# A list of its own for the first batch: who accumulates y in units 0 to 12

## The chip, the cores and the metric

One core of a Trainium2 chip. The metric is the device time of one execution, in microseconds (us); lower is better. The engines of the core are named as the profile names them: PE (TensorE, with PEld its weight loads), DVE (VectorE), ACT (ScalarE), POOL (GpSimd) and SP (SyncE, which here only issues DMAs).

## The reference

Four batches of 512 time steps go through a selective state-space layer beside a gated feed-forward layer. Cut to what matters here (D = 1024 channels, N = 16 states, H = 512):

```python
xn = layernorm(x)
u, gate = split(xn @ W_in.T); u = silu(causal_conv(u))
dt, B, C = rmsnorm each of split(u @ Wx.T)
delta = softplus(dt @ Wdt.T + dt_bias)
state[d, n] = exp(delta[d] * A[d, n]) * state[d, n] + delta[d] * u[d] * B[n]   # for each time step
y[d] = sum over n of state[d, n] * C[n]
s = ((y + u * D_param) * silu(gate)) @ W_out.T
g = silu(down(silu(gate_ffn(xn)) * up(xn)))
out = x + s * g
```

The change touches only who adds up the sum over n that gives y.

## The kernel before

The batches run one after the other: batch 0 written out on its own, batches 1 and 2 in a loop, batch 3 written out on its own (`sequences`). Inside a batch the scan is cut into 32 **units** (`UNITS`): unit i is state n = i mod 16 of channel half i // 16, which is four tiles of 128 channels by 512 time steps. A unit has two **slots**, so a batch has 64 slots, and every engine's program is written slot by slot with other work (feed-forward, projections, the next batch's preparation) placed in fixed slots.

What one unit costs on each engine:

- POOL makes `dBu` = v times B, one instruction per slot (L794), into a ring of three buffers: the one of slot s waits for the scans of slot s - 3.
- ACT makes the decays `dA` = exp(delta A) in PSUM, two per slot (L584).
- DVE scans, two per slot (L1018): `dA` and `dBu` in, the state `h` out. It waits for both.
- PE transposes `h` back to time-major, 128 time steps (an index c from 0 to 3) at a time, into two PSUM banks hT0 (c = 0 and 2) and hT1 (c = 1 and 3) (L1364). c = 0, 1 go in the unit's first slot and c = 2, 3 in its second, and each waits until the bank's former contents were read. PE's slots run one to two behind DVE's, because the first waits for all four scans of its unit.
- y, in `yT`, gets hT times C[n] added. DVE does it in one instruction per c (`add_state`, L947; L941 where n = 0), in the two slots of the next unit, behind that slot's scans and ahead of its other work. For some (unit, c) it is **handed over**: ACT multiplies the bank by C[n] into a buffer `part` of SBUF (`take_state`, L677; with n = 0 straight into `yT`), and POOL adds that to `yT` (`add_part`, L764), four slots after the unit's start.

`handed_over(u)` says which: c = 0 of nearly all units, and c = 2 as well in units 11 to 22. The same list holds for all four batches. OFF is the list of these, OFF_ADDS those of them with n > 0, ON all others; counts of them (`done_by`) are the values that the semaphores ev_done (ACT), yp_done (POOL) and y_done (DVE) are waited for.

Batch 0 differs from the others in one thing: the weights that feed the fp32r products (x is multiplied in a high and a low part, L1079) are split there, once, and kept in DRAM for the later batches. ACT rounds an entry to its high part (`round_w`, L449) and POOL subtracts to get the low part (`rest_w`, L733). 15 entries are split inside the slots of batch 0: on POOL in the even slots 2 to 26, then in slots 33 and 36. PE's product of slot 2t (feed-forward, t = 0 to 10) waits for the low part made in POOL's slot 2t + 2. In slots 14, 16, 18 and 20 POOL has one more instruction of 128x1024 each (L744 or L749, for the second channel half), and in slot 25 eleven short ones for the next batch's layer norm (L702 to L719).

Of the kernel before, what the change touches and what calls it, by code (L numbers as in the profile page):

```python
# [11 lines left out]
JH = KD // HF  # L12
UNITS = N * HF
# [70 lines left out]
def done_by(acts, u, c):  # L84

    return len([a for a in acts if a <= (u, c)])

# [45 lines left out]
def build(nc, x, w_ring, w_x, w_dt, conv_w, conv_b, a_par, d_par, ln_w, ident_d, out):  # L133
# [5 lines left out]
    with ctx:  # L139
# [287 lines left out]
        def _(act):  # L427
# [146 lines left out]
            def sequence(b, first, last):  # L574
# [88 lines left out]

                def take_state(c_b, i, c, no_first):

                    hf, n = i // N, i % N
                    act.wait_ge(hT_ps, c_b * UNITS * TC + i * TC + c + 1)
                    if n == 0:
                        if not no_first:
                            act.wait_ge(yb_ps, (c_b - 1) * KD + (hf + 1) * JH)  # L670
                        dst = yT[:, c, hf * JH * P:(hf + 1) * JH * P]
                    else:
                        q = OFF_ADDS.index((i, c))
                        if not (no_first and q < 2):
                            act.wait_ge(yp_done, c_b * len(OFF_ADDS) + q - 1)
                        dst = part[:, q % 2, :]
                    nc.scalar.activation(dst, hT[c % H_BANKS][:, :], ACT.Copy, scale=cs_act[:, c, n:n + 1]).then_inc(ev_done, 1)  # L677

                for s in range(SLOTS):
                    decay(s)  # L680
                    side(s)
                    for i, c in OFF:
                        if s == 2 * i + 2 + c // 2:
                            take_state(b, i, c, first)
                        elif s == 2 * i + 2 + c // 2 - SLOTS and not first:
                            take_state(b - 1, i, c, False)
# [9 lines left out]
        def _(pool):  # L696
# [57 lines left out]

            def add_part(c_b, i, c):
                q, hf = OFF_ADDS.index((i, c)), i // N
                pool.wait_ge(ev_done, c_b * len(OFF) + done_by(OFF, i, c))
                before = [p for p in range(q) if OFF_ADDS[p][1] == c and OFF_ADDS[p][0] // N == hf]
                if (i - 1, c) in ON:
                    pool.wait_ge(y_done, c_b * len(ON) + done_by(ON, i - 1, c))  # L760
                elif before:
                    pool.wait_ge(yp_done, c_b * len(OFF_ADDS) + before[-1] + 1)
                y = yT[:, c, hf * JH * P:(hf + 1) * JH * P]
                nc.gpsimd.tensor_tensor(y, y, part[:, q % 2, :], ALU.add).then_inc(yp_done, 1)  # L764

# [11 lines left out]
            def sequence(b, first, last):  # L777
                for s in range(SLOTS):
# [20 lines left out]
                    if s in LO_AT and first:  # L799
                        o, k = LO_AT[s]  # L800
                        rest_w(slot_of(b, k), o % HI_RING, split(k))
                    for m, c in OFF_ADDS:
                        if s == 2 * m + 4 + c // 2:
                            add_part(b, m, c)
                        elif s == 2 * m + 4 + c // 2 - SLOTS and not first:
                            add_part(b - 1, m, c)
                    j = s - S_YB1 - 7 + JH
# [25 lines left out]
            sequences(pool, sequence)  # L833
            for m, c in OFF_ADDS:
                if SLOTS <= 2 * m + 4 and m < UNITS - 1:
                    add_part(NB - 1, m, c)
            for j in range(JH, KD):
# [3 lines left out]
        def _(dve):  # L841
# [91 lines left out]
            def sequence(b, first, last):  # L933
                def add_state(c_b, i, c):
# [3 lines left out]
                    dve.wait_ge(hT_ps, c_b * UNITS * TC + i * TC + c + 1)  # L938
                    if n == 0:
                        dve.wait_ge(cs_done, c_b + 1)  # L940
                        nc.vector.tensor_scalar(y, hT[c % H_BANKS][:, :], cn, None, ALU.mult).then_inc(y_done, 1)  # L941
                    else:
                        if (i - 1, c) in ON:
                            dve.wait_ge(y_done, c_b * len(ON) + done_by(ON, i - 1, c))
                        else:
                            dve.wait_ge(yp_done, c_b * len(OFF_ADDS) + done_by(OFF_ADDS, i - 1, c))
                        nc.vector.scalar_tensor_tensor(out=y, in0=hT[c % H_BANKS][:, :], scalar=cn, in1=y,  # L947
                                                       op0=ALU.mult, op1=ALU.add).then_inc(y_done, 1)
# [3 lines left out]
                def side(s):  # L952
                    if first and 1 <= s < 3:
                        gate_silu(0, s + 1, pj[s - 1])
                    if s == 1 and not first:
                        dve.wait_ge(y_done, b * len(ON))
                        hand_c(b)
# [54 lines left out]
                for s in range(SLOTS):  # L1012
                    i, part = s // 2, s % 2
                    dve.wait_ge(dBu_done, b * SLOTS + s + 1)
                    for e in range(2):
                        g = 2 * s + e
                        dve.wait_ge(dA_done, b * SCANS + g + 1)
                        nc.vector.tensor_tensor_scan(h[:, i % 2, 2 * part + e, :], dA[g % 2][:, :], dBu[:, dbu_buffer(s), e, :],  # L1018
                                                     0.0, ALU.mult, ALU.add).then_inc(scan_done, 1)
                    for c in (2 * part, 2 * part + 1):  # L1020
                        if i > 0 and (i - 1, c) in ON:
                            add_state(b, i - 1, c)
                        elif i == 0 and not first and (UNITS - 1, c) in ON:
                            add_state(b - 1, UNITS - 1, c)
                    side(s)
# [3 lines left out]
            for c in range(TC):  # L1029
                i = UNITS - 1  # L1030
                dve.wait_ge(hT_ps, b * UNITS * TC + i * TC + c + 1)
                if (i - 1, c) in ON:
                    dve.wait_ge(y_done, b * len(ON) + done_by(ON, i - 1, c))
                else:
                    dve.wait_ge(yp_done, (b + 1) * len(OFF_ADDS) - len(handed_over(i)) - len(handed_over(i - 1)) + done_by([(i - 1, d) for d in handed_over(i - 1)], i - 1, c))
                y = yT[:, c, JH * P:D]
# [13 lines left out]
        def _(pe):  # L1050
# [88 lines left out]
            def sequence(b, first, last):  # L1139
# [209 lines left out]
                for s in range(SLOTS):  # L1349
# [3 lines left out]
                    for c in (2 * part, 2 * part + 1):  # L1353

                        before = (i, c - H_BANKS) if c >= H_BANKS else (i - 1, c + TC - H_BANKS)
                        if not first or before[0] >= 0:
                            if last and before[0] == UNITS - 1:
                                pe.wait_ge(y_done, b * len(ON) + done_by(ON, UNITS - 2, TC) + before[1] + 1)
                            elif before in ON or (UNITS - 1, before[1]) in ON and before[0] < 0:
                                pe.wait_ge(y_done, b * len(ON) + (done_by(ON, *before) if before[0] >= 0 else done_by(ON, UNITS - 1, before[1]) - len(ON)))  # L1360
                            else:
                                pe.wait_ge(ev_done, b * len(OFF) + (done_by(OFF, *before) if before[0] >= 0 else done_by(OFF, UNITS - 1, before[1]) - len(OFF)))
                        for j in range(JH):
# [24 lines left out]
            for c in range(TC):  # L1388

                pe.wait_ge(y_done, b * len(ON) + done_by(ON, UNITS - 2, TC) + c + 1)  # L1390
                for j in (JH, JH + 1):
# [76 lines left out]
```

## Time and profile before

| | |
|---|---|
| median of 3 runs | 1181.65 us (1178.9 to 1184.5) |
| profiled execution | 1188.98 us, its span 1186.9 us |
| busy: PE, DVE, POOL, ACT | 90%, 86%, 86%, 60% of the span |
| slots of batch 0 | from 65 us to 358 us |
| granted TensorE clock, mean | 0.961 |

The start of DVE's scans tells where a slot lies in the trace: slot 4 at 87.20 us, slot 12 at 121.82, slot 14 at 131.57, slot 21 at 169.19, slot 28 at 200.86, slot 34 at 224.52. A timeline row gives start, duration of the row's instructions together (one begins a little before the one ahead of it has ended, so the distance of starts is the smaller price), the engine, line, tiles, shapes, the count, and in brackets how long the engine had been idle and what ended that.

### The profile page before, as it was taken

To read this page: it belongs to the slowest core of one execution; us is meant where nothing else is said; L and a number is where in the kernel's file an instruction comes from. 1 tells how busy PE (TensorE), PEld (TensorE's weight loads), DVE (VectorE), ACT (ScalarE), POOL (GpSimd) and SP (SyncE) were. 2 spreads that over 40 slices of the span, in tenths; PEclk is the share of its full clock that TensorE was granted. 3 is DMA by queue.
4 is the path that set the end of the run, shared out by engine and by line. 5 is a ranking of instruction groups with operands and counts; after the bars stand their busy time and mean duration, and the time that the engine had idled before them with its cause. 6 is when DMAs were issued, how large, how long until landed. Compare 5 with 4: busy or idle time off the path is not lost.

```text
span 1186.9 us, 16724 instructions
## 1 busy us (share of the span) xinstructions
PE 1070.9 (90%) x5072; PEld 766.5 (65%) x5072; DVE 1026.3 (86%) x1217; ACT 711.3 (60%) x1155; POOL 1016.0 (86%) x586
## 2 busy tenths in 40 slices
PE   5979987889999999998997999998998999999767
PEld 4747766666757776675855787576756777555444
DVE  3469788899789999899986999899998999888895
ACT  4657646776475756477583565576576575565440
POOL 3679999999878899889987789879998889889961
PEclk9979999799799999999998999999999999999878
DMA  3627654443223543343322364324333443334310
GB/s 126 214 94 242 215 169 159 147 146 133 63 90 140 190 164 141 132 151 134 99 90 101 133 215 163 131 98 157 118 100 105 162 155 130 109 114 169 124 62 36
DMA packets 46570, 160.86 MB, mean 136 GB/s; under 512 B 5355, under 2 KB 5611, under 8 KB 37004
## 3 DMA queue, kind: packets, MB, share of 16 engines
q1 hardware_dynamic: 45424, 159.14, 38.7%
q8 instruction: 44, 0.72, 0.2%
q10 hardware_dynamic: 1052, 0.59, 0.2%
q14 instruction: 50, 0.41, 0.1%
HBM read 135.33 MB, written 24.38 MB: 135 GB/s over the span
## 4 chain that ended last, share of the span: by engine, by line
PE 49%; DVE 17%; POOL 16%; issue 13%; ACT 3%; DVEq 1%; DMA 1%; SPq 0%; POOLq 0%; ACTq 0%
PE pj L1079 16%; PE hT L1364 10%; DVE sb_h L1018 8%; POOL sb_dBu L794 8%; PE pj L1277 7%; PE pj L1311 5%; DVE sb_yT L947 4%; PE pj L1342 3%; POOL sb_yT L764 3%; PE pj L1084 2%; PE pj L1382 2%; DVE sb_un L872 2%; PE pj L1097 2%; POOL sb_w_sp L733 1%; POOL sb_un L738 1%
## 5 line engine op out<-in xcount | busy, mean ns | idle before, releaser
L1018 DVE TENSOR_TENSOR_SCAN sb_h<-dA,sb_dBu 128x512 f32<-128x512 f32 x512 | 596.8, 1207 | 43.7 <-POOL sb_dBu L794 30.2
L794 POOL TENSOR_TENSOR sb_dBu<-sb_v,sb_bb 128x1024 f32<-128x1024 f32 x256 | 607.1, 2384 | 28.6 <-DVE sb_h L1018 22.8
L584 ACT ACTIVATE dA<-sb_delta,sb_apar 128x512 f32<-128x512 f32 x512 | 344.9, 688 | 232.4 <-DVE sb_h L1018 226.4
L1079 PE MATMUL pj<-sb_x_hi,sb_w_sp 128*128 128x512 f32 x1208 | 345.8, 410 | 25.4 <-DVE sb_un L872 12.3
L1364 PE MATMUL hT<-sb_ident,sb_h 128*128 128x128 f32 x2048 | 288.7, 283 | 66.8 <-DVE sb_yT L947 51.7
L1364 PEld LDWEIGHTS hT<-sb_ident,sb_h 128*128 128x128 f32 x2048 | 244.4, 145 | 149.9 <-issue 50.9
L1079 PEld LDWEIGHTS pj<-sb_x_hi,sb_w_sp 128*128 128x128 f32 x1208 | 221.2, 193 | 89.0 <-issue 24.6
L947 DVE SCALAR_TENSOR_TENSOR sb_yT<-hT,sb_cs,sb_yT 128x512 f32<-128x512 f32 x321 | 229.2, 735 | 53.8 <-PE hT L1364 53.2
L764 POOL TENSOR_TENSOR sb_yT<-sb_yT,sb_part 128x512 f32<-128x512 f32 x155 | 199.4, 1286 | 63.5 <-ACT sb_part L677 63.4
L677 ACT ACTIVATE sb_part<-hT,sb_cs_act 128x512 f32<-128x512 f32 x155 | 106.1, 685 | 161.4 <-PE hT L1364 152.9
L1079 PE MATMUL pj<-sb_x_lo,sb_w_sp 128*128 128x512 f32 x604 | 167.4, 400 | 0.0
L1079 PEld LDWEIGHTS pj<-sb_x_lo,sb_w_sp 128*128 128x128 f32 x604 | 117.4, 194 | 27.8
L1311 PE MATMUL pj<-sb_S,sb_ring 128*128 128x512 f32 x264 | 121.8, 598 | 0.0
L1277 PE MATMUL pj<-sb_u,sb_ring 128*128 128x512 f32 x192 | 86.6, 594 | 0.0
L1311 PEld LDWEIGHTS pj<-sb_S,sb_ring 128*128 128x128 f32 x264 | 46.8, 190 | 52.7 <-issue 52.7
L872 DVE SCALAR_TENSOR_TENSOR sb_un<-pj,sb_cw,sb_un 128x511 f32<-128x511 f32 (+2 forms) x93 | 69.5, 747 | 4.9 <-ACT sb_un L478 2.7
L733 POOL TENSOR_TENSOR sb_w_sp<-sb_ring,sb_w_sp 128x1024 fp32r<-128x1024 f32 x21 | 49.9, 2377 | 19.2 <-ACT sb_w_sp L449 19.2
L1277 PEld LDWEIGHTS pj<-sb_u,sb_ring 128*128 128x128 f32 x192 | 34.6, 190 | 35.0 <-issue 34.6
L753 POOL TENSOR_TENSOR sb_u<-sb_u,sb_sgate 128x512 f32<-128x512 f32 x32 | 41.4, 1297 | 11.3 <-DVE sb_u L899 11.3
L749 POOL TENSOR_TENSOR sb_v<-sb_delta,sb_un 128x1024 f32<-128x1024 f32 x16 | 38.1, 2383 | 8.7 <-DVE sb_delta L925 8.3
L744 POOL TENSOR_TENSOR sb_delta<-sb_delta,sb_v 128x1024 f32<-128x1024 f32 x14 | 33.4, 2388 | 11.1 <-ACT sb_v L534 11.1
L738 POOL TENSOR_TENSOR sb_un<-sb_v,sb_un 128x512 f32<-128x512 f32 x32 | 41.4, 1300 | 0.0
(126 smaller groups left out, 810.1 us busy)
## 6 DMA issues: line engine op xcount, KB each, us to landing
sb_w_sp<-w_cache SPq DMA_DIRECT2D x55, 1024.0 KB, 4.8
sb_ring<-w_ring SPq DMA_DIRECT2D x67, 512.0 KB, 3.3
sb_bb<-b_rows SPq DMA_DIRECT2D x128, 256.0 KB, 3.6
w_cache<-sb_w_sp SPq DMA_DIRECT2D x19, 1024.0 KB, 4.9
sb_xio<-x SPq DMA_DIRECT2D x7, 1024.0 KB, 6.9
out<-sb_xio SPq DMA_DIRECT2D x3, 1024.0 KB, 5.6
sb_xio<-x SPq DMA_DIRECT2D x4, 256.0 KB, 3.6
out<-sb_xio SPq DMA_DIRECT2D x4, 256.0 KB, 2.0
```

The lines of the kernel that those rows point to most:

```text
L584: nc.scalar.activation(dA[g % 2][:, :], delta[:, j, :], ACT.Exp, scale=apar[:, j, n:n + 1]).then_inc(dA_done, 1)
L677: nc.scalar.activation(dst, hT[c % H_BANKS][:, :], ACT.Copy, scale=cs_act[:, c, n:n + 1]).then_inc(ev_done, 1)
L733: nc.gpsimd.tensor_tensor(w_lo[:, buf], ring[:, slot], w_hi[:, buf].bitcast(fp32), ALU.subtract).then_inc(lo_done, 1)
L764: nc.gpsimd.tensor_tensor(y, y, part[:, q % 2, :], ALU.add).then_inc(yp_done, 1)
L794: nc.gpsimd.tensor_tensor(dBu[:, dbu_buffer(s), :, :], v[:, j:j + 2, :], bb[:, i % B_RING, :].unsqueeze(1).to_broadcast([P, 2, T]), ALU.mu ...
L872: nc.vector.scalar_tensor_tensor(out=acc[:, k:T], in0=bank[:, 0:T - k], scalar=cw[:, j, KC - 1 - k:KC - k], in1=acc[:, k:T], op0=ALU.mult, ...
L947: nc.vector.scalar_tensor_tensor(out=y, in0=hT[c % H_BANKS][:, :], scalar=cn, in1=y, op0=ALU.mult, op1=ALU.add).then_inc(y_done, 1)
L1018: nc.vector.tensor_tensor_scan(h[:, i % 2, 2 * part + e, :], dA[g % 2][:, :], dBu[:, dbu_buffer(s), e, :], 0.0, ALU.mult, ALU.add).then_in ...
L1079: done = nc.tensor.matmul(bank[:, :], w[:, kk * P:(kk + 1) * P], xs[:, kk, :], start=(p == 0), stop=(p == len(products) - 1))
L1277: done = nc.tensor.matmul(pj[e % 2][:, :], ring[:, slot_of(b, OUT0 + e), part, m * P:(m + 1) * P], u[:, j, :], start=(j == 0), stop=(j == ...
L1311: done = nc.tensor.matmul(pj[DOWN_BANK[e]][:, :], ring[:, slot_of(b, DOWN0 + x3 // 2), x3 % 2, t % 4 * P:(t % 4 + 1) * P], S[:, t, :], sta ...
L1364: done = nc.tensor.transpose(hT[c % H_BANKS][:, j * P:(j + 1) * P], h[:, i % 2, j, c * P:(c + 1) * P], ident[:, :])
```

## The change

`handed_over` gets a second argument, whether this is batch 0. There, units 0 to 12 hand nothing over: DVE does all four c of them. From unit 13 on, and in batches 1 to 3, the list is as it was. So in batch 0 fifteen pairs (c = 0 of units 0 to 12, c = 2 of units 11 and 12) move: 15 instructions of ACT and 14 of POOL go, 15 of DVE come. PE waits for y_done where it waited for ev_done. The rest of the diff is bookkeeping of the counts, which differ between batch 0 and the others now; in the loop they come to as many register instructions as before, give or take one. The buffer of `part` is now counted from the list's end.

```diff
-def handed_over(u):
-    return (0, 2) if 11 <= u < 23 else () if u in (29, 30) else (0,)
-
-
-OFF = [(u, c) for u in range(UNITS) for c in handed_over(u)]
-OFF_ADDS = [(u, c) for u, c in OFF if u % N > 0]
-ON = [(u, c) for u in range(UNITS) for c in range(TC) if (u, c) not in OFF]
+def handed_over(u, first):
+    return () if u in (29, 30) or first and u < FIRST_UNIT else (0, 2) if 11 <= u < 23 else (0,)
+
+
+FIRST_UNIT = 13
+OFF, OFF_ADDS, ON = {}, {}, {}
+for first in (True, False):
+    OFF[first] = [(u, c) for u in range(UNITS) for c in handed_over(u, first)]
...
+def total(acts, b):
+
+    return 0 if isinstance(b, int) and b == 0 else b * len(acts[False]) + len(acts[True]) - len(acts[False])
...
-                    for i, c in OFF:
+                    for i, c in OFF[first]:
                         if s == 2 * i + 2 + c // 2:
-                            take_state(b, i, c, first)
+                            take_state(i, c, False)
...
-                    for m, c in OFF_ADDS:
+                    for m, c in OFF_ADDS[first]:
                         if s == 2 * m + 4 + c // 2:
-                            add_part(b, m, c)
+                            add_part(b, m, c, False)
...
-                        if i > 0 and (i - 1, c) in ON:
-                            add_state(b, i - 1, c)
+                        if i > 0 and c not in handed_over(i - 1, first):
+                            add_state(i - 1, c, False)
```

POOL around slots 14 to 16 of batch 0 (L733 is the low part of the weights, L764 the addition to y, L744 and L749 the extra work of these slots, L794 the dBu of two slots). Before:

```order
L733 TENSOR_TENSOR sb_w_sp<-sb_ring,sb_w_sp 128x1024
L764 TENSOR_TENSOR sb_yT<-sb_yT,sb_part 128x512
L744 TENSOR_TENSOR sb_delta<-sb_delta,sb_v 128x1024
L794 TENSOR_TENSOR sb_dBu<-sb_v,sb_bb 128x1024 x2
L733 TENSOR_TENSOR sb_w_sp<-sb_ring,sb_w_sp 128x1024
L764 TENSOR_TENSOR sb_yT<-sb_yT,sb_part 128x512
L749 TENSOR_TENSOR sb_v<-sb_delta,sb_un 128x1024
```

POOL at the same place after the change (its lines are 17 to 20 further on in the file):

```order
L750 TENSOR_TENSOR sb_w_sp<-sb_ring,sb_w_sp 128x1024
L761 TENSOR_TENSOR sb_delta<-sb_delta,sb_v 128x1024
L814 TENSOR_TENSOR sb_dBu<-sb_v,sb_bb 128x1024 x2
L750 TENSOR_TENSOR sb_w_sp<-sb_ring,sb_w_sp 128x1024
L766 TENSOR_TENSOR sb_v<-sb_delta,sb_un 128x1024
```

The addition to y between the weights' low part and the next work is gone.

DVE in an even and an odd slot of the same place (the rows on sb_h are the scans, those on sb_S the feed-forward). Before:

```order
L1018 SCALAR_TENSOR_TENSOR sb_h<-dA,sb_dBu 128x512 x2
L947 SCALAR_TENSOR_TENSOR sb_yT<-hT,sb_cs,sb_yT 128x512
L964 SCALAR_TENSOR_TENSOR sb_S<-sb_S,pj 128x512
L1018 SCALAR_TENSOR_TENSOR sb_h<-dA,sb_dBu 128x512 x2
L947 SCALAR_TENSOR_TENSOR sb_yT<-hT,sb_cs,sb_yT 128x512 x2
L969 SCALAR_TENSOR_TENSOR sb_S<-sb_S,pj 128x512
```

DVE at the same place after the change:

```order
L1041 SCALAR_TENSOR_TENSOR sb_h<-dA,sb_dBu 128x512 x2
L970 SCALAR_TENSOR_TENSOR sb_yT<-hT,sb_cs,sb_yT 128x512 x2
L987 SCALAR_TENSOR_TENSOR sb_S<-sb_S,pj 128x512
L1041 SCALAR_TENSOR_TENSOR sb_h<-dA,sb_dBu 128x512 x2
L970 SCALAR_TENSOR_TENSOR sb_yT<-hT,sb_cs,sb_yT 128x512 x2
L992 SCALAR_TENSOR_TENSOR sb_S<-sb_S,pj 128x512
```

The even slot holds two accumulations where it held one; the new one, c = 0, stands ahead of c = 1.

PE in an odd slot, with what the instructions wait for. Before:

```order
L1364 MATMUL hT0<-sb_ident,sb_h 128x128 [waits ev_done]
L1364 MATMUL hT0<-sb_ident,sb_h 128x128 x3
L1364 MATMUL hT1<-sb_ident,sb_h 128x128 [waits y_done]
L1364 MATMUL hT1<-sb_ident,sb_h 128x128 x3
L1079 MATMUL pj0<-sb_x_hi,sb_w_sp 128x512 [waits fs_done]
```

PE at the same place after the change:

```order
L1391 MATMUL hT0<-sb_ident,sb_h 128x128 [waits y_done]
L1391 MATMUL hT0<-sb_ident,sb_h 128x128 x3
L1391 MATMUL hT1<-sb_ident,sb_h 128x128 [waits y_done]
L1391 MATMUL hT1<-sb_ident,sb_h 128x128 x3
L1102 MATMUL pj0<-sb_x_hi,sb_w_sp 128x512 [waits fs_done]
```

Nothing moved; bank hT0 is now waited for on DVE (y_done) and no more on ACT (ev_done).

## Rows read from the trace of the kernel before

**Rows 1.** The page's first part: span, and busy time by engine.
```profile
span 1186.9 us, 16724 instructions
PE 1070.9 (90%) x5072; PEld 766.5 (65%) x5072; DVE 1026.3 (86%) x1217; ACT 711.3 (60%) x1155; POOL 1016.0 (86%) x586
```

**Rows 2.** Busy time by stretch of batch 0; PEclk is the granted clock.
```profile
85.00:130.00 45.00, 45.00 (x230) 35.16 (x228) 39.13 (x46) 35.05 (x55) 41.95 (x21) 1.00 0.72 245
130.00:168.00 38.00, 31.73 (x148) 24.31 (x147) 28.30 (x34) 18.89 (x27) 38.00 (x19) 0.91 0.55 181
168.00:206.00 38.00, 31.08 (x160) 24.46 (x158) 33.49 (x40) 23.41 (x37) 37.53 (x30) 0.96 0.47 162
228.00:293.00 65.00, 58.16 (x282) 41.29 (x280) 64.30 (x76) 48.93 (x79) 65.00 (x41) 1.00 0.43 151
```

**Rows 3.** Timeline of POOL in slot 16.
```profile
139.65 2.36 POOL L733 TENSOR_TENSOR sb_w_sp<-sb_ring,sb_w_sp 128x1024 fp32r<-128x1024 f32 x1
141.98 1.27 POOL L764 TENSOR_TENSOR sb_yT<-sb_yT,sb_part 128x512 f32<-128x512 f32 x1
143.22 2.38 POOL L749 TENSOR_TENSOR sb_v<-sb_delta,sb_un 128x1024 f32<-128x1024 f32 x1
```

**Rows 4.** DVE's waits at 130:168, 168:206, 206:228: us, times, longest.
```profile
DVE sb_h L1018 <- POOL sb_dBu L794: 8.1, 3, 2.9
...
DVE sb_h L1018 <- POOL sb_dBu L794: 6.1, 3, 2.8
...
DVE sb_h L1018 <- POOL sb_dBu L794: 2.6, 1, 2.6
```

**Rows 5.** Timeline of DVE: slots 12, 13, 17, 26 and 27.
```profile
124.07 0.73 DVE L947 SCALAR_TENSOR_TENSOR sb_yT<-hT,sb_cs,sb_yT 128x512 f32<-128x512 f32 x1
...
127.42 2.34 DVE L1018 TENSOR_TENSOR_SCAN sb_h<-dA,sb_dBu 128x512 f32<-128x512 f32 x2 [2.03 <-ACT dA L584]
129.68 1.38 DVE L947 SCALAR_TENSOR_TENSOR sb_yT<-hT,sb_cs,sb_yT 128x512 f32<-128x512 f32 x2
...
147.98 2.34 DVE L1018 TENSOR_TENSOR_SCAN sb_h<-dA,sb_dBu 128x512 f32<-128x512 f32 x2 [2.88 <-POOL sb_dBu L794]
...
191.35 2.34 DVE L1018 TENSOR_TENSOR_SCAN sb_h<-dA,sb_dBu 128x512 f32<-128x512 f32 x2 [0.96 <-POOL sb_dBu L794]
...
197.24 2.34 DVE L1018 TENSOR_TENSOR_SCAN sb_h<-dA,sb_dBu 128x512 f32<-128x512 f32 x2 [2.30 <-POOL sb_dBu L794]
```

**Rows 6.** Timeline of ACT in slots 12 and 13.
```profile
124.65 0.67 ACT L677 ACTIVATE sb_part<-hT,sb_cs_act 128x512 f32<-128x512 f32 x1
125.33 1.28 ACT L584 ACT_TABLE_LOAD   x1
...
127.87 1.03 ACT L449 CAST sb_w_sp<-sb_ring 128x1024 fp32r<-128x1024 f32 x1
```

**Rows 7.** PE's first gap after 85 us; who waited for L947 (us, times).
```profile
130.55 1.22 PE L1364 MATMUL hT<-sb_ident,sb_h 128*128 128x128 f32 x8 [0.25 <-DVE sb_yT L947]
```
```profile
  PE hT L1364: 51.7, 37
```

**Rows 8.** Timeline from slot 32 to 34: ACT, POOL, DVE.
```profile
216.38 0.69 ACT L677 ACTIVATE sb_part<-hT,sb_cs_act 128x512 f32<-128x512 f32 x1 [1.31 <-PE hT L1364]
216.97 1.04 ACT L449 CAST sb_w_sp<-sb_ring 128x1024 fp32r<-128x1024 f32 x1
```
```profile
218.57 2.34 POOL L733 TENSOR_TENSOR sb_w_sp<-sb_ring,sb_w_sp 128x1024 fp32r<-128x1024 f32 x1
```
```profile
224.52 2.34 DVE L1018 TENSOR_TENSOR_SCAN sb_h<-dA,sb_dBu 128x512 f32<-128x512 f32 x2 [2.56 <-POOL sb_dBu L794]
```

**Rows 9.** Timeline of PE: the products with Wx in batch 0 and batch 1.
```profile
293.00 4.68 PE L1084 MATMUL pj<-sb_wx,sb_un 128*128 128x64 f32 x32 [1.37 <-POOL sb_un L738]
...
299.18 6.93 PE L1084 MATMUL pj<-sb_wx,sb_un 128*128 128x64 f32 x32
...
575.07 3.68 PE L1084 MATMUL pj<-sb_wx,sb_un 128*128 128x64 f32 x32
```

More of the change, by code:

```diff
@@ L71, with done_by, done_before @@
 LO_AT = {q + 2: (o, k) for o, k, q in MADE}
-def handed_over(u):
-    return (0, 2) if 11 <= u < 23 else () if u in (29, 30) else (0,)
-OFF = [(u, c) for u in range(UNITS) for c in handed_over(u)]
-OFF_ADDS = [(u, c) for u, c in OFF if u % N > 0]
-ON = [(u, c) for u in range(UNITS) for c in range(TC) if (u, c) not in OFF]
-def done_by(acts, u, c):
-    return len([a for a in acts if a <= (u, c)])
+def handed_over(u, first):
[4 more added lines that the diff above has]
+    OFF[first] = [(u, c) for u in range(UNITS) for c in handed_over(u, first)]
+    OFF_ADDS[first] = [(u, c) for u, c in OFF[first] if u % N > 0]
+    ON[first] = [(u, c) for u in range(UNITS) for c in range(TC) if (u, c) not in OFF[first]]
+def total(acts, b):
+    return 0 if isinstance(b, int) and b == 0 else b * len(acts[False]) + len(acts[True]) - len(acts[False])
+def done_by(acts, b, u, c):
+    return total(acts, b) + len([a for a in acts[isinstance(b, int) and b == 0] if a <= (u, c)])
+def done_before(acts, b, u, c):
+    return total(acts, b) - len([a for a in acts[False] if a > (u, c)])
 def dbu_buffer(s):
@@ L753, in times_gate, with add_part @@
                 nc.gpsimd.tensor_tensor(u[:, j, :], u[:, j, :], sgate[:, j, :], ALU.mult).then_inc(yg_done, 1)
[L755 to L760, printed above, removed]
+            def add_part(b, i, c, carried):
+                acts = OFF_ADDS[isinstance(b, int) and b == 0 and not carried]
+                q, hf = acts.index((i, c)), i // N
+                done = done_before if carried else done_by
+                pool.wait_ge(ev_done, done(OFF, b, i, c))
+                before = [a for a in acts[:q] if a[1] == c and a[0] // N == hf]
+                if i > 0 and c not in handed_over(i - 1, acts is OFF_ADDS[True]):
+                    pool.wait_ge(y_done, done(ON, b, i - 1, c))
                 elif before:
-                    pool.wait_ge(yp_done, c_b * len(OFF_ADDS) + before[-1] + 1)
+                    pool.wait_ge(yp_done, done(OFF_ADDS, b, *before[-1]))
                 y = yT[:, c, hf * JH * P:(hf + 1) * JH * P]
-                nc.gpsimd.tensor_tensor(y, y, part[:, q % 2, :], ALU.add).then_inc(yp_done, 1)
+                nc.gpsimd.tensor_tensor(y, y, part[:, (len(acts) - q) % 2, :], ALU.add).then_inc(yp_done, 1)
             power_ln(0)
@@ L937, in add_state @@
                     cn = cs[:, c, n:n + 1]
-                    dve.wait_ge(hT_ps, c_b * UNITS * TC + i * TC + c + 1)
+                    dve.wait_ge(hT_ps, b * UNITS * TC + (i - UNITS if carried else i) * TC + c + 1)
                     if n == 0:
-                        dve.wait_ge(cs_done, c_b + 1)
+                        dve.wait_ge(cs_done, b + 1)
                         nc.vector.tensor_scalar(y, hT[c % H_BANKS][:, :], cn, None, ALU.mult).then_inc(y_done, 1)
                     else:
-                        if (i - 1, c) in ON:
-                            dve.wait_ge(y_done, c_b * len(ON) + done_by(ON, i - 1, c))
+                        done = done_before if carried else done_by
+                        if c not in handed_over(i - 1, first and not carried):
+                            dve.wait_ge(y_done, done(ON, b, i - 1, c))
+                        elif (i - 1) % N == 0:
+                            dve.wait_ge(ev_done, done(OFF, b, i - 1, c))
                         else:
-                            dve.wait_ge(yp_done, c_b * len(OFF_ADDS) + done_by(OFF_ADDS, i - 1, c))
+                            dve.wait_ge(yp_done, done(OFF_ADDS, b, i - 1, c))
                         nc.vector.scalar_tensor_tensor(out=y, in0=hT[c % H_BANKS][:, :], scalar=cn, in1=y,
@@ L955, in side @@
                     if s == 1 and not first:
-                        dve.wait_ge(y_done, b * len(ON))
+                        dve.wait_ge(y_done, total(ON, b))
                         hand_c(b)
@@ L1020, in sequence @@
                     for c in (2 * part, 2 * part + 1):
-                        if i > 0 and (i - 1, c) in ON:
-                            add_state(b, i - 1, c)
-                        elif i == 0 and not first and (UNITS - 1, c) in ON:
-                            add_state(b - 1, UNITS - 1, c)
+                        if i > 0 and c not in handed_over(i - 1, first):
+                            add_state(i - 1, c, False)
+                        elif i == 0 and not first and c not in handed_over(UNITS - 1, False):
+                            add_state(UNITS - 1, c, True)
                     side(s)
@@ L1031, in _ @@
                 dve.wait_ge(hT_ps, b * UNITS * TC + i * TC + c + 1)
-                if (i - 1, c) in ON:
-                    dve.wait_ge(y_done, b * len(ON) + done_by(ON, i - 1, c))
+                if c not in handed_over(i - 1, False):
+                    dve.wait_ge(y_done, done_by(ON, b, i - 1, c))
                 else:
-                    dve.wait_ge(yp_done, (b + 1) * len(OFF_ADDS) - len(handed_over(i)) - len(handed_over(i - 1)) + done_by([(i - 1, d) for d in handed_over(i - 1)], i - 1, c))
+                    dve.wait_ge(yp_done, done_by(OFF_ADDS, b, i - 1, c))
                 y = yT[:, c, JH * P:D]
@@ L1357, in sequence @@
                             if last and before[0] == UNITS - 1:
-                                pe.wait_ge(y_done, b * len(ON) + done_by(ON, UNITS - 2, TC) + before[1] + 1)
-                            elif before in ON or (UNITS - 1, before[1]) in ON and before[0] < 0:
-                                pe.wait_ge(y_done, b * len(ON) + (done_by(ON, *before) if before[0] >= 0 else done_by(ON, UNITS - 1, before[1]) - len(ON)))
+                                pe.wait_ge(y_done, done_by(ON, b, UNITS - 2, TC) + before[1] + 1)
+                            elif before[0] < 0 and before[1] in handed_over(UNITS - 1, False):
+                                pe.wait_ge(ev_done, done_before(OFF, b, UNITS - 1, before[1]))
+                            elif before[0] < 0:
+                                pe.wait_ge(y_done, done_before(ON, b, UNITS - 1, before[1]))
+                            elif before[1] in handed_over(before[0], first):
+                                pe.wait_ge(ev_done, done_by(OFF, b, *before))
                             else:
-                                pe.wait_ge(ev_done, b * len(OFF) + (done_by(OFF, *before) if before[0] >= 0 else done_by(OFF, UNITS - 1, before[1]) - len(OFF)))
+                                pe.wait_ge(y_done, done_by(ON, b, *before))
                         for j in range(JH):
@@ L1388, in _ @@
             for c in range(TC):
[L1390 removed]
+                pe.wait_ge(y_done, done_by(ON, b, UNITS - 2, TC) + c + 1)
                 for j in (JH, JH + 1):
```

39 lines of the change are left out of this document (21 added, 18 removed).

## The prediction

> **What bounds the kernel now.** I read the page's totals first: PE 90%, DVE and POOL 86% each [rows 1]. No engine is the bound of the whole, so what a change in batch 0 is worth must be read there. The second view, busy time by stretch, cuts batch 0 by its limits [rows 2]. From 85 to 130 us (slots 3 to 13) PE has no gap at all: 45.00 of 45.00 us. From 130 to 168 (slots 14 to 20) POOL is full, 38.00 of 38.00, while PE has 31.73 and DVE 28.30. From 168 to 206 POOL has 37.53, DVE 33.49. From 228 to 293 POOL (65.00) and DVE (64.30) are both full. So the change takes work from the engine that sets the pace from 130 us on, and does so for 13 units, but of these units seven lie where PE sets the pace.
>
> The third view is who waits: DVE's scans wait for POOL's dBu for 8.1 us in the second stretch, 6.1 in the third and 2.6 in the piece from 206 to 228 [rows 4]. These waits are what can be won, less what DVE gets to do.
>
> **Prices.** One addition on POOL is 143.22 - 141.98 = 1.24 us from start to start [rows 3]; 14 of them go, 17.4 us of POOL. One accumulation on DVE is 0.73 us alone and two are 1.38, so one more is 0.65 [rows 5]; 15 come, 9.8 us of DVE. One take-over on ACT is 125.33 - 124.65 = 0.68 us [rows 6]; 15 go, 10.2 us of ACT.
>
> **Slots 2 to 12: nothing.** PE is full up to 130.3 us, and its first gap is the 0.25 us ahead of 130.55 [rows 7]. What goes from POOL and ACT here is not on the path. What comes on DVE, six accumulations of 0.65 by slot 12, has cover: DVE was busy for 39.13 of 45.00 us [rows 2], and the new instruction often fits into a wait, because it needs only c = 0, which PE transposes ahead of the c = 1 that DVE was waiting for. The new wait of PE (bank hT0 on DVE and no longer on ACT) stands in front of one that was there: c = 3 waits for DVE's c = 1 of the same slot anyway. PE's odd slot starts its transposes after DVE has done its even slot's accumulations with some 1 to 3 us to spare, as I lay the slots out from the rows. If that cover is gone, each of seven units costs up to the wait that PE has for L947 on average, 51.7 / 37 = 1.4 us [rows 7]; I take 0, and keep both ends.
>
> **Slot 13: 0.7 us.** DVE waits 2.03 us for a decay of ACT [rows 5]. In front of that decay stand a take-over and a load of the function table. The take-over goes: 0.68 us sooner [rows 6]. The rounding at 127.87 comes sooner by as much, and so does POOL's split behind it, which waited for it. DVE's new accumulation in slot 12 lies inside the rest of the 2.03 us. Bounds: 0, if DVE is late by then, and 1.0, if ACT is early further back too. I take 0.7, because nothing else stands between these rows.
>
> **Slots 14 to 20: 5.0 us.** POOL is full without a gap. In each of the slots 14, 16, 18 and 20 it does a split, an addition, and one more 128x1024 instruction before the dBu of the odd slot, for which DVE then waits, 2.88 us at 147.98 [rows 5] and 2.7 on average of the three in rows 4. The addition goes: 4 x 1.24 = 5.0 us. What is late next is DVE, which gets 0.65 us more in each even slot, against a wait of over 2 us per unit, of which 1.24 goes: 2.88 - 1.24 - 0.65 = 1.0 us is left, so POOL stays the bound. PE has 31.7 of 38 us, and 33 us is what is left: it has little room, but some. So far 5.7 us, at slot 21.
>
> **Slots 21 to 28: 0.** Here DVE becomes the bound. It gets five more accumulations (slots 22, 24, 25, 26, 27): +3.25 us. It loses the waits of 0.96 and 2.30 us for dBu in slots 26 and 27 [rows 5], since POOL is rid of three more additions in front of the dBu of slot 27, 3.7 us, and goes ahead: -3.26. Bounds: POOL's work in front of slot 27 is two splits and the layer norm of the next batch, all fixed; if these waits stay, it is 3.3 us worse.
>
> **Slots 29 to 63: 0.5 us.** The work is the same as before. POOL is ahead now, but the 2.56 us that DVE waits in slot 34 don't go with that: the split in front (218.57) needs the rounding on ACT (216.97, ends at 218.01), which stands behind a take-over that waits for PE, which waits for DVE's own scans of slot 31 [rows 8]. Of this only POOL's own lateness goes, 218.57 - 218.01 = 0.56. Then DVE and POOL are both full up to 293 [rows 2] and carry the gain on, and PE after them.
>
> **Sum.** 0.7 + 5.0 + 0 + 0.5 = 6.2 us. Batches 1 to 3 have the same instructions as before and begin 6.2 us sooner. Of the profiled execution, 1188.98 becomes 1182.8 us. That execution was 7.3 us over the median of the runs shown; I take the same difference off the median: 1181.65 - 6.2 = 1175.4 us, 0.52% less.
>
> **Rivals.**
> *The bank goes free later (slower).* Up to 130 us PE is the path, and its wait for hT0 is moved from ACT, 60% busy, to DVE. For: the new accumulation stands ahead of c = 1, so the second bank goes free 0.65 us later too. Against: the 1 to 3 us to spare. Priced at 1.4 us for each of seven units it costs 9.8, less the 6.2 gained: 1181.65 + 3.6 = 1185.3 us. It decides once PE's odd slots before 130 us show a gap for L947 on average of over 0.9 us, where there was none.
>
> *DVE is at its limit (slower).* If DVE sets the pace all through, all 15 are on the path: 15 x 0.65 = 9.8 us, 1191.4 us. The waits of rows 4 speak against it, 14.2 us in which DVE has nothing to do in just the slots that get nine of the new instructions. The Trainium skill (Perfetto Trace Analysis, "Optimizing Scalar/DVE Operations") advises handing work to ScalarE, or even GpSimd, where VectorE is saturated, and this change does the contrary with a VectorE that is 86% busy; by that rule it would be this rival's time. The trace bears it out for 228 to 293 us, where nothing is moved, and not for 130 to 206.
>
> *Half of it (same).* The waits of slots 26 and 27 stay, because they come from the layer norm and the splits and not from the additions: 6.2 - 3.3 = 2.9, 1178.8 us.
>
> *More (faster).* In batch 0 PE waits 1.37 us before the products with Wx, and the second 32 of them take 6.93 us where batch 1 has 3.68 [rows 9]; the granted clock is lower there. If POOL's lead lets them begin without the gap, 1.37 + (4.68 - 3.68) + (6.93 - 3.68) = 5.6 us come on top: 1169.8 us. Against: POOL and DVE are both full before it, so the gap moves with them.
>
> *Nothing is moved* I hold for excluded: the built program shows the fifteen accumulations on DVE, and PE's wait on y_done.
>
> **Chances.** The forecast (a gain of 4.5 to 8 us) 0.47, half 0.24, more 0.14, later banks 0.10, DVE at its limit 0.05. A measurement can tell about 0.5% from no change, here 5.9 us, and the forecast of 6.2 lies just past it. Of the forecast I put 0.32 over and 0.15 under it. Faster by more: 0.32 + 0.14 = 0.46. Slower by more: 0.05 and 0.02 of the later banks, 0.07. The rest, 0.47, within. The range runs from 1169.0 (the larger gain) to 1185.5 (the later banks) and leaves out DVE at its limit and the ends of both sides.
>
> **What would show it.** POOL's splits in slots 14 to 22 come 1.24 us closer together. DVE's wait for dBu at 130 to 168 shrinks from 8.1 to some 3 us, and goes at slots 26 and 27. The scans of slot 14 begin within 1 us of 131.57, those of slot 21 at 163.5, of slot 28 at 195.2, of slot 34 at 218.3; the products with Wx at 286.8 instead of 293.00. A gap on PE before 130 us would speak for the later banks, scans of slot 28 at 198 for the half. It would be wrong altogether if batches 1 to 3 didn't carry the gain on, or if the granted clock of PE fell where it now waits on DVE.

## The result and the profile after

| | before | after |
|---|---|---|
| median | 1180.79 us (9 runs) | 1175.53 us (9 runs) |
| ratio to before | | 0.9942, 95% interval 0.9922 to 0.9962 |
| profiled execution, its span | 1188.98, 1186.9 us | 1172.87, 1171.1 us |
| busy DVE, POOL, ACT | 1026.3, 1016.0, 711.3 us | 1035.4, 998.4, 702.6 us |

The forecast was 1175.4 us, 6.2 us less than the median then known. The ratio comes to 6.8 us less (4.5 to 9.2 us by its interval); the two medians alone lie 5.3 us apart.

The two profiled executions are 15.8 us apart, over twice as much. So the first thing to learn from the traces is where each microsecond lies. The starts of DVE's scans serve as milestones, since every slot has them:

| stretch of batch 0 | before | after | difference |
|---|---|---|---|
| slot 4 to 12 | 34.62 | 34.64 | 0.0 |
| slot 12 to 14 | 9.75 | 8.86 | -0.9 |
| slot 14 to 21 | 37.62 | 32.75 | -4.9 |
| slot 21 to 28 | 31.67 | 31.36 | -0.3 |
| slot 28 to 48 | 85.60 | 84.95 | -0.65 |
| slot 48 to 56 | 38.36 | 32.53 | -5.8 |
| slot 12 to 48 in all | 164.64 | 157.92 | -6.7 |

From slot 12 to slot 48 it is 6.7 us, in the main the working of the prediction. Of the other 9.1 us, 5.8 lie in slots 48 to 56, 2.8 in the rest of batch 0 and in the later batches, where no instruction was changed, and 0.5 ahead of slot 4.

The page of the changed kernel, its span and totals (before: [rows 1]):

```profile
span 1171.1 us, 16696 instructions
PE 1062.0 (91%) x5072; PEld 757.3 (65%) x5072; DVE 1035.4 (88%) x1232; ACT 702.6 (60%) x1140; POOL 998.4 (85%) x572
```

Its busy time by stretch, in the columns of [rows 2] (PE, PEld, DVE, ACT, POOL; then granted clock, DMA share, GB/s):

```profile
85.00:130.00 45.00, 45.00 (x230) 35.26 (x229) 42.96 (x52) 32.32 (x49) 36.38 (x17) 1.00 0.69 229
130.00:168.00 38.00, 32.97 (x169) 25.16 (x168) 34.61 (x43) 17.04 (x24) 38.00 (x18) 1.00 0.58 195
168.00:206.00 38.00, 31.34 (x160) 23.16 (x158) 38.00 (x47) 23.04 (x36) 35.39 (x27) 0.96 0.48 159
```

To be seen: up to 130 us PE is still at 45.00 of 45.00, and POOL has merely become idle (41.95 to 36.38). From 130 to 168 POOL is still the full one. From 168 to 206 the full one is now DVE, 38.00 of 38.00, and POOL has room.

DVE's timeline in the changed kernel: the first scans of slots 13, 17, 26, 27 and 34:

```profile
126.05 2.34 DVE L1041 TENSOR_TENSOR_SCAN sb_h<-dA,sb_dBu 128x512 f32<-128x512 f32 x2 [0.48 <-ACT dA L598]
...
144.15 2.34 DVE L1041 TENSOR_TENSOR_SCAN sb_h<-dA,sb_dBu 128x512 f32<-128x512 f32 x2 [1.01 <-POOL sb_dBu L814]
...
186.03 2.35 DVE L1041 TENSOR_TENSOR_SCAN sb_h<-dA,sb_dBu 128x512 f32<-128x512 f32 x2
...
190.17 2.35 DVE L1041 TENSOR_TENSOR_SCAN sb_h<-dA,sb_dBu 128x512 f32<-128x512 f32 x2
...
216.33 2.34 DVE L1041 TENSOR_TENSOR_SCAN sb_h<-dA,sb_dBu 128x512 f32<-128x512 f32 x2 [1.00 <-POOL sb_dBu L814]
```

Against [rows 5]: the wait for ACT went from 2.03 to 0.48 us, that for POOL in slot 17 from 2.88 to 1.01 (forecast: 1.0), and those of slots 26 and 27 are gone. The 2.56 us of slot 34 [rows 8] are 1.00 in this trace; part of that moved to a wait for PE behind it, below.

POOL in slot 16 of the changed kernel, against [rows 3]; the addition between the two is gone:

```profile
137.04 2.37 POOL L750 TENSOR_TENSOR sb_w_sp<-sb_ring,sb_w_sp 128x1024 fp32r<-128x1024 f32 x1
139.38 2.39 POOL L766 TENSOR_TENSOR sb_v<-sb_delta,sb_un 128x1024 f32<-128x1024 f32 x1
```

### The profile page after: what moved, and what is told of

It is laid out like the page before. It is cut to its first block, busy times and chain, and to the rows that moved or that the text cites. A ratio compares the mean times of both kernels' runs of the same rounds, so it can differ in the third digit from the quotient of the medians.

```text
span 1171.1 us, 16696 instructions
## 1 busy us (share of the span) xinstructions
PE 1062.0 (91%) x5072; PEld 757.3 (65%) x5072; DVE 1035.4 (88%) x1232; ACT 702.6 (60%) x1140; POOL 998.4 (85%) x572
## 4 chain that ended last, share of the span: by engine, by line
PE 52%; DVE 20%; issue 12%; POOL 11%; ACT 4%; DVEq 1%; DMA 0%; SPq 0%; POOLq 0%; ACTq 0%
PE pj L1102 18%; PE hT L1391 11%; DVE sb_h L1041 10%; PE pj L1300 7%; POOL sb_dBu L814 5%; DVE sb_yT L970 5%; PE pj L1334 5%; PE pj L1365 3%; PE pj L1120 2%; DVE sb_un L892 2%; PE pj L1409 2%; PE pj L1107 2%; POOL sb_yT L784 2%; POOL sb_un L755 1%; POOL sb_v L766 1%
## 5 line engine op out<-in xcount | busy, mean ns | idle before, releaser
L970 DVE SCALAR_TENSOR_TENSOR sb_yT<-hT,sb_cs,sb_yT 128x512 f32<-128x512 f32 x335 | 239.3, 740 | 43.8 <-PE hT L1391 43.2
L784 POOL TENSOR_TENSOR sb_yT<-sb_yT,sb_part 128x512 f32<-128x512 f32 x141 | 181.2, 1285 | 57.6 <-ACT sb_part L694 57.4
L694 ACT ACTIVATE sb_part<-hT,sb_cs_act 128x512 f32<-128x512 f32 x141 | 96.4, 684 | 139.6 <-PE hT L1391 138.0
```

The source lines that it names most:

```text
L784: nc.gpsimd.tensor_tensor(y, y, part[:, (len(acts) - q) % 2, :], ALU.add).then_inc(yp_done, 1)
```

## The experiments

Theory: POOL's relief is worth its price only in slots 14 to 20, where POOL is the bound; DVE's new work is free up to slot 20 and then just as large as the waits that it takes the place of. Rivals: DVE is at its limit everywhere; PE's banks go free later; POOL's total work is what counts; the granted clock makes the difference.

In all of them "12 to 48" is the distance of the scans of slot 12 and slot 48 in batch 0. It doesn't hold what happens before PE's full stretch, nor the products with Wx from slot 47's end on. It is 164.64 before and 157.92 after.

**The kernel before, a second trace** (no edit).

> The kernel before, unchanged, for a second trace. The two traces shown differ by 15.8 us in span, the medians by 5.3. Theory: the schedule moves by 7 us up to slot 48 of batch 0, and the rest of the 15.8 is the granted clock of the single execution (the two groups of products with Wx in batch 0: 4.68 and 6.93 us in the one trace, 3.79 and 3.68 in the other). Then this trace has the same slot distances as the first up to slot 48, and may well have 3.8 and 3.7 us for the two groups. Rival: the low clock there is a property of the kernel before; then 4.7 and 6.9 us come again.

Measured: 12 to 48 in 164.86 us, 0.2 more than in the first trace; span 1180.8 us, 6.1 us less than the first. PE's timeline at the products with Wx:

```profile
294.65 3.79 PE L1084 MATMUL pj<-sb_wx,sb_un 128*128 128x64 f32 x32 [1.43 <-POOL sb_un L738]
...
299.16 3.68 PE L1084 MATMUL pj<-sb_wx,sb_un 128*128 128x64 f32 x32
```

They take 3.79 and 3.68 us, as in batch 1, where the first trace had 4.68 and 6.93 [rows 9], and behind nearly the same gap (1.43 us here, 1.37 there). The stretch from 291 to 308 us in the first trace, and then in this one:

```profile
291.00:308.00 17.00, 15.63 (x87) 15.33 (x86) 10.00 (x13) 5.61 (x10) 17.00 (x10) 0.64 0.29 97
```

```profile
291.00:308.00 17.00, 15.57 (x118) 14.37 (x118) 14.75 (x18) 7.25 (x14) 17.00 (x11) 1.00 0.28 93
```

The granted clock is 0.64 in the one and 1.00 in the other, with the same program. Slots 48 to 56 take 32.52 us in this trace, where the first has 38.36 and the changed kernel 32.53. So 5.8 us of the 15.8 are no property of either kernel. By that the second difference, 1180.8 - 1171.1 = 9.7 us of span, is nearer to what the timings say, and 6.9 of it lies in slots 12 to 48.

**The changed kernel again**, twice, on other occasions (no edit).

> The changed kernel, unchanged, timed again. Theory: a gain of 6 to 7 us in each execution, ratio 0.9945 (0.992 to 0.997). Its trace has the scans of slot 4 to slot 48 of batch 0 within 1 us of 192.6 us apart. Rival (the clock gives the gain): the two groups of products with Wx keep to 3.8 and 3.7 us in every trace of this kernel, and the ratio goes to 0.989.

> The changed kernel for the comparison with the one above: ratio 0.9944, slots 12 to 48 157.2 to 157.9 us apart.

Measured: ratios 0.9944 (0.9923 to 0.9965) and 0.9938 (0.9909 to 0.9967); 12 to 48 in 157.16 and 157.19 us. Slot 4 to 48 is 191.8 us. The Wx products took 3.79 and 3.68 us both times. Of thirteen traces in this study ten have these values; one of before (4.68 and 6.93) and two of changed versions, below, have more. Of the rival's two signs the first came true (3.8 and 3.7 us in every trace of this kernel) and the second didn't: the ratio stayed where it was and did not go to 0.989. Both values occur with either kind of list, so the clock at this place doesn't separate the kernels. How often each kernel meets the low clock can't be told from two and three traces; but the ratio's 6.8 us agree with the 6.7 to 7.7 us of slots 12 to 48, so there is little left for it to explain.

**Relief without DVE's new work.** 14 of the 15 new accumulations do 8 of 512 columns, so y lacks the rest of them.

```diff
+                        w = 8 if first and not carried and i < FIRST_UNIT and c in handed_over(i, False) else T
-                        nc.vector.scalar_tensor_tensor(out=y, in0=hT[c % H_BANKS][:, :], scalar=cn, in1=y,
+                        nc.vector.scalar_tensor_tensor(out=y[:, 0:w], in0=hT[c % H_BANKS][:, 0:w], scalar=cn, in1=y[:, 0:w],
```

> As the changed kernel, but 14 of the 15 new accumulations on DVE do only 8 of their 512 columns, so y is incomplete: the relief of POOL nearly without DVE's new work. Theory: in slots 14 to 20 POOL is the bound, so nothing more is won there; in slots 22 to 27 DVE is the bound, so 5 x 0.5 = 2.5 us more than in the changed kernel, slot 28 begins about 2.5 us sooner; ratio 0.992. Rival (DVE is at its limit all through): 14 x 0.5 = 7 us more, ratio 0.988. Rival (POOL's relief is worth nothing by itself): no more than 0.994.

Measured: slot 21 comes 41.57 us after slot 12, where the changed kernel has 41.61: nothing more is won while POOL is the bound. Slot 28 comes at 70.33 against 72.97, 2.6 us sooner, and slot 48 at 154.77, 2.4 to 3.15 sooner than in the three traces of the changed kernel. An accumulation and a thin one together take 0.85 us where two take 1.39, so 5 x 0.54 = 2.7 is what was left out in slots 22 to 27. The timed ratio, 0.9941 (0.9913 to 0.9969), doesn't show these 2.6 us: it was to be 0.992, which its interval just holds. Its own trace loses 5.1 us in batch 3, 1.7 in each of slots 24 to 32, 32 to 40 and 40 to 48, and the second and third traces of the changed kernel lose 3.2 to 3.3 in the last two of these, each at a granted clock of 0.95 where the first trace of the changed kernel has 1.00. So the clock later in the execution is larger than the 2.6 us, and a timing can't separate them. Both rivals fall by the slots: not 7 us, and not nothing.

**DVE's new work without the relief.** The kernel before with 14 more accumulations that nobody reads, on c = 1 (and c = 3) of the same units.

```diff
+                        if first and c_b is b and i < 13 and (c == 1 or c == 3 and i > 10):
+                            nc.vector.scalar_tensor_tensor(out=junk[:, :], in0=hT[c % H_BANKS][:, :], scalar=cn, in1=y,
+                                                           op0=ALU.mult, op1=ALU.add)
```

> The kernel before, with 14 more accumulations on DVE in units 1 to 12 whose result (bf16) nobody reads; POOL and ACT keep theirs. DVE's new work without the relief. Theory: it all fits into DVE's waits for PE, ACT and POOL, which are 19 us between slot 6 and slot 28: 0 to 2 us, ratio 1.000 to 1.002. Rival (DVE is at its limit): 14 x 0.65 = 9.1 us, ratio 1.0077. Rival (the banks go free later): PE shows gaps for L947 before 130 us, up to 9.8 us, ratio up to 1.008.

Measured: 12 to 48 in 164.55 us (before 164.64 and 164.86), slot 4 to 12 in 34.63 (34.62): 9.1 us of DVE work cost nothing by the time slot 48 comes. On the way slots 21 to 28 take 0.5 us more (32.21 against 31.67 and 31.60), and slots 31 to 36 give it back. The ratio is 1.0021 (1.0004 to 1.0038), 0.5 to 4.5 us, where up to 2 were expected. The trace has two of the 1.7 us losses at a lower clock in batch 3; whether they have to do with the new work is open. The rival's price of 9 us is excluded. DVE's waits from 93 to 206 us in this kernel (us, times, longest):

```profile
DVE sb_h L1022 <- POOL sb_dBu L795: 9.0, 5, 2.3
DVE sb_h L1022 <- ACT dA L585: 1.4, 1, 1.4
```

The 14.2 us of the same wait in [rows 4] became 9.0: the waits give way to the work. No wait of PE for DVE appears from 85 us to 131.44, where PE waits 0.23 us, so the banks don't go free too late either. "DVE is at its limit" falls for slots up to 21, and for slots 21 to 28 as long as POOL makes DVE wait there.

**Only units 0 to 4, and only units 5 to 12.**

```diff
-FIRST_UNIT = 13
+FIRST_UNIT = 5
```

> Only units 0 to 4 keep all their accumulations on DVE; their five pairs lie in slots 2 to 12, where PE has no gap. Theory: nothing: slots 12 to 48 stay 164.6 us apart as in the kernel before, ratio 1.000 (0.998 to 1.002). Rival (what counts is POOL's total work): 4 x 1.24 = 5.0 us, ratio 0.996.

```diff
-    return () if u in (29, 30) or first and u < FIRST_UNIT else (0, 2) if 11 <= u < 23 else (0,)
+    return () if u in (29, 30) or first and 5 <= u < FIRST_UNIT else (0, 2) if 11 <= u < 23 else (0,)
```

> Only units 5 to 12, ten pairs. Theory: the whole gain of the changed kernel: slots 12 to 48 are 157 to 158 us apart, ratio 0.9944. Rival (POOL's total work counts): ten of fourteen additions, 5 us, ratio 0.996.

Measured: 0.9989 (0.9968 to 1.0011) and 12 to 48 in 164.69 us for the first; 0.9927 (0.9899 to 0.9956) and 157.51 us for the second. Five of the thirteen units bring nothing, the other eight bring all; the rival's 0.996 lies outside both intervals. In the first of the two, POOL and PE show why. POOL's splits of slots 8 and 12, with the additions gone (the one of slot 10 waits 2.88 us):

```profile
99.28 2.35 POOL L750 TENSOR_TENSOR sb_w_sp<-sb_ring,sb_w_sp 128x1024 fp32r<-128x1024 f32 x1 [1.28 <-ACT sb_w_sp L463]
...
118.89 2.40 POOL L750 TENSOR_TENSOR sb_w_sp<-sb_ring,sb_w_sp 128x1024 fp32r<-128x1024 f32 x1 [2.63 <-ACT sb_w_sp L463]
```

POOL waits for ACT's rounding, for 1.28 to 2.88 us. Before the change its additions filled most of this wait (0.58 us are left in slot 10 and 1.45 in slot 12), so taking them away only lengthens it. And PE is full:

```profile
85.00:130.00 45.00, 45.00 (x229) 35.05 (x228) 41.63 (x50) 32.79 (x50) 35.91 (x16) 1.00 0.69 231
```

Slot 13 shows how the 0.9 us there are made up. It comes 5.60 us after slot 12 before, 5.28 with units 0 to 4 alone, 5.02 with units 5 to 12 alone, and 4.71 with both: 0.3 from the earlier take-overs and 0.6 from units 5 and up, whose first take-over (unit 5, slot 12) stands right in front, and they add up.

The trace of the second is also one of the three with a low clock at the products with Wx: 6.16 and 3.80 us, behind a gap of 1.40 us. The third is the second trace of the version with units 0 to 11, below: 5.99 and 3.96 us behind 1.33.

**More units, 0 to 15.**

```diff
-FIRST_UNIT = 13
+FIRST_UNIT = 16
```

> Units 13 to 15 too: six pairs more go from ACT and POOL to DVE, in DVE's slots 28 to 33. In the changed kernel DVE has no gap from slot 22 to slot 33 and 1.0 us in slot 34. Theory: DVE is the bound there, 6 x 0.65 - 1.0 = 2.9 us slower than the changed kernel at slot 36, slots 12 to 48 about 160.5 us apart, ratio 0.997. Rival (POOL is the bound in all of batch 0): 6 x 1.24 = 7.4 us faster than the changed kernel.

Measured: 0.9972 (0.9936 to 1.0009), 12 to 48 in 160.76 us. POOL has 7.4 us less to do than in the changed kernel, and slot 48 comes 2.8 us later than in the changed kernel's first trace (3.6 than in the others). The timed ratio, whose interval holds both 1 and the changed kernel's 0.9942, can't tell this; the slots do, and the rival, 7.4 us faster, falls. DVE's scans of slots 33 and 34, with no idle time ahead of them:

```profile
215.42 2.33 DVE L1041 TENSOR_TENSOR_SCAN sb_h<-dA,sb_dBu 128x512 f32<-128x512 f32 x2
...
218.97 2.33 DVE L1041 TENSOR_TENSOR_SCAN sb_h<-dA,sb_dBu 128x512 f32<-128x512 f32 x2
```

**Fewer units: 0 to 11, and 0 to 10.**

```diff
-FIRST_UNIT = 13
+FIRST_UNIT = 12
```

> Without unit 12: its two pairs stay with ACT and POOL. Theory: DVE is the bound in slots 26 and 27, so slot 28 begins 2 x 0.65 = 1.3 us sooner than in the changed kernel, and POOL still has enough lead; slots 12 to 48 about 156.2 us apart, ratio 0.993, no difference from the changed kernel that a timing could tell. Rival (POOL is the bound there): two additions of 1.24 us later, 2.5 us slower than the changed kernel.

> The version without unit 12 again, beside the changed kernel on the same chip. Theory: the same slots, 12 to 48 in 156.5 us, 1.2 us less than the changed kernel, so ratios of 0.993 and 0.994, which the timings can't tell apart.

```diff
-FIRST_UNIT = 13
+FIRST_UNIT = 11
```

> Units 11 and 12 keep their old list: four pairs stay with ACT and POOL. Theory: the two engines change places as the bound. DVE has 4 x 0.65 = 2.6 us less to do, so slot 28 comes at 71.0 us after slot 12 (73.0 in the changed kernel, 71.7 without unit 12), but POOL now has 5.0 us more in front of its split of slot 33, uses up its lead and is late there: slot 34 is back to within 0.5 us of the changed kernel, slots 12 to 48 157.0 to 157.9 us apart. Rival (DVE alone is the bound from slot 21 on): 2.6 us sooner all the way, 154.9 to 155.3.

Measured:

| units that DVE keeps | slot 28 after slot 12 | slot 48 after slot 12 | ratio (95%) |
|---|---|---|---|
| none (before) | 79.04 | 164.64 | 1 |
| 0 to 10 | 71.43 | 156.96 | 0.9922 (0.9888 to 0.9955) |
| 0 to 11 | 71.68, again 71.65 | 156.51, again 155.85 | 0.9910 (0.9871 to 0.9949), again 0.9904 (0.9873 to 0.9936) |
| 0 to 12 (the change) | 72.97, 72.99, 73.03 | 157.92, 157.16, 157.19 | 0.9942, 0.9944, 0.9938 |
| 0 to 15 | 72.99 | 160.76 | 0.9972 (0.9936 to 1.0009) |

Without unit 12 slot 28 comes 1.3 us sooner, as worked out from 2 x 0.65. Without units 11 and 12 it comes only 0.25 sooner still (I had expected 0.7, but DVE waits 0.89 us for POOL in slot 27), and the lead is gone by slot 34, where DVE waits for POOL as long as before the change: slot 34 comes 95.04 us after slot 12, in the changed kernel 94.99 to 95.26, in the version with units 0 to 11 93.76 and 93.91. DVE's scan of slot 34 in that version:

```profile
215.05 2.34 DVE L1041 TENSOR_TENSOR_SCAN sb_h<-dA,sb_dBu 128x512 f32<-128x512 f32 x2 [2.55 <-POOL sb_dBu L814]
```

So of these four lists the best ends at unit 11: one unit further DVE is the bound, one unit less POOL is. The gain over the change as made is 1.3 us by the slots. In the timings on one chip the version with units 0 to 11 has 0.9904 and the change 0.9938, a difference that points the same way and is larger, but the intervals overlap; I count the 1.3 us as shown and no more. It has the lowest ratios of all versions here, and by the slots it is the fastest of those that compute all of y.

## Why the prediction was right, point by point

**Slots 2 to 12, 0 forecast, 0.0 measured.** PE stayed at 45.00 of 45.00 us, and slots 4 to 12 took 34.64 us against 34.62. (The prediction counted seven units here; units 0 to 4 are the ones whose take-overs all lie ahead of slot 12, and unit 5's, in slot 12, already counts for slot 13.) The wait on bank hT0 moved from ACT to DVE and cost nothing: PE's first wait for DVE after 85 us is at 137.89 in the changed kernel, later than before [rows 7]:

```profile
137.89 1.23 PE L1391 MATMUL hT<-sb_ident,sb_h 128*128 128x128 f32 x8 [0.40 <-DVE sb_yT L970]
```

That excludes the rival of the later banks. Units 0 to 4 alone confirm the zero from the other side. Twelve of the thirteen traces have 34.60 to 34.64 us here, whatever the list; the first one with units 0 to 11 has 33.68, and why is open.

**Slot 13, 0.7 forecast, 0.9 measured.** The bound of 1.0 that I had set was nearer. The rest is that ACT is early further back too: with the take-overs of units 0 to 4 alone gone, slot 13 comes 0.3 us sooner.

**Slots 14 to 20, 5.0 forecast, 4.9 measured.** Four additions of 1.24 us, and the wait left in slot 17 was worked out as 1.0 and is 1.01.

**Slots 21 to 28, 0 forecast, 0.2 to 0.3 measured.** DVE took over as the bound, as the thin accumulations and the lists of different length show. "Half of it" falls: the waits of slots 26 and 27 are gone, not kept.

**Slots 29 to 63, 0.5 forecast, 0.65 to 1.7 measured.** This term was too small, because [rows 8] were misread. Up to slot 31 hardly anything changes (slot 28 to 31 takes 11.05 us after, 11.16 before). From slot 31 to slot 34 the kernel before takes 12.50 and 12.47 us in its two traces, the changed kernel 10.97, 11.17 and 11.18: 1.3 to 1.5 us less, and not 0.56. The prediction held that the rounding in front of POOL's split stands behind a take-over that waits for PE, so that only POOL's own lateness could go. The second trace of the kernel before shows what the take-over waited for; POOL's addition, which frees its buffer `part`, and then the take-over:

```profile
216.33 1.27 POOL L764 TENSOR_TENSOR sb_yT<-sb_yT,sb_part 128x512 f32<-128x512 f32 x1
...
217.69 0.69 ACT L677 ACTIVATE sb_part<-hT,sb_cs_act 128x512 f32<-128x512 f32 x1 [1.28 <-POOL sb_yT L764]
```

In the first trace POOL's addition ended at 216.29, PE's group of eight transposes at 216.37, and the take-over began at 216.38; the row names PE because its group ended last, though the take-over needs only the first four of the eight (c = 0). With POOL ahead, in the second trace of the changed kernel, only PE is left to wait for:

```profile
207.65 0.69 ACT L694 ACTIVATE sb_part<-hT,sb_cs_act 128x512 f32<-128x512 f32 x1 [0.48 <-PE hT L1391]
```

The take-over starts 3.5 us after the scans of slot 31, where it started 4.4 after them: 0.8 us on top of POOL's own 0.5.

From slot 34 to 36 the second and third traces of the changed kernel take 8.73 us, as the first one of before, but the first takes 9.72. There PE is at a low clock for longer: a group of four products takes 1.78 us that takes 1.10 at the same place of the second trace, and DVE waits for the transposes behind it:

```profile
216.83 1.78 PE L1102 MATMUL pj<-sb_x_hi,sb_w_sp 128*128 128x512 f32 x4
```
```profile
219.52 0.75 DVE L961 TENSOR_SCALAR sb_yT<-hT,sb_cs 128x512 f32<-128x512 f32 x1 [0.85 <-PE hT L1391]
```

I had left the clock out of this term. Then DVE and POOL are both full and carry everything on: slots 36 to 48 take 53.20 or 53.21 us in every trace of both kernels.

**The later batches** carry the gain on, as forecast. Batch 1 even takes 0.6 to 0.7 us less (271.0 us in all three traces of the changed kernel, 271.6 and 271.7 before), nearly all of it in DVE's last wait for POOL in that batch (2.61 us in the first trace, before 3.26); its cause is open. Batches 2 and 3 vary by up to 1.8 and 2.0 us between traces of one kernel.

**The sum, 6.2 forecast, 6.7 to 7.7 by the slots, 6.8 by the ratio.** The bounds were right in every stretch up to slot 31, with the change from POOL to DVE at slot 21, and what the wait of slot 34 hangs on was misread. The sizes were off by 0.2 (slot 13), -0.1 (slots 14 to 20), 0.3 (slots 21 to 28) and 0.15 to 1.2 us (slots 29 to 63). That the median came out within 0.2 us of the forecast 1175.4 is luck: the nine executions of the changed kernel spread over 9 us.

**"More"** named the right place, the products with Wx, and the wrong reason. They did run faster in the first trace of the changed kernel, by the very 0.9 and 3.3 us, but the gap ahead of them stayed (1.41 us, forecast: it moves along), and the kernel before does the same in its second trace.

**The rule of the Trainium skill** (Perfetto Trace Analysis, "Optimizing Scalar/DVE Operations") is that handing work away may make sense if VectorE is saturated. It agrees with these runs where the rows of the stretch show saturation: six pairs moved on to DVE in slots 28 to 33, where it has no gap, cost about 3 us by the slots. Where DVE waits, 14 more accumulations cost nothing up to slot 21 and 0.5 us up to slot 28. Had the 86% of the whole span been read as saturation, the rule would have spoken against this change, with the rival's 1191.4 us; 1175.53 us were measured.

## What to carry to other kernels

An engine's work is worth its price only in the stretch in which it is the bound, so cut a one-off phase (here the batch that splits the weights) into stretches by who has no idle time, and give it a list of its own. When work is moved between two engines, the new list should end where the waits of the receiving engine end: six pairs too many (units 13 to 15) cost about 3 us of the 7. A row puts a wait down to whatever ended last; where two releasers end within 0.1 us of each other, as ahead of the take-over of slot 32, look up in the kernel what the instruction waits for, or look at a second trace, before you decide what a change will leave in place. Milestones in the trace, starts of the same instruction in both kernels, separate a change of 7 us from 9 us of chance in single executions; totals don't.

## What the runs showed of the hardware that I had not expected

The same program, at the same place and behind a gap of nearly the same length (1.33 to 1.51 us), had its 64 small products with Wx at a granted clock of 1.00 in ten traces and at a lower one in three (0.64 over 17 us in one of them), which cost about 2.5 to 5.8 us by slot 56. What decides it is open; it wasn't the kernel's order of work, since the kernel before shows both.

Batch 3 has such places too. Its slots 24 to 32, 32 to 40 and 40 to 48 take 31.1, 32.7 and 30.1 us at a granted clock of 1.00, and 1.5 to 1.7 us more at 0.95. Both traces of the kernel before, the one with units 0 to 4, the first of the changed kernel and the one with units 5 to 12 have none of these losses, the other eight have two or three. That is seven of the nine traces in which units 5 to 12, or most of them, were moved, none of the three in which they weren't, and the one with DVE's extra work. It may be chance; if it isn't, the change loses a part of its gain to the clock later on. This is open too.
